# Attention kernel on one core: the dense product of a duo stands behind its last two maxima, and its copy behind the relu

## The reference, cut to what matters

```python
xn = layernorm(x)                                   # over the 256 columns
q = relu(xn @ Wq.T + bq)                            # keys k and values v likewise, once for all batches
score = einsum('bhsd,bhtd->bhst', qh, kh) / 4       # 16 heads of 16 columns
a = softmax(score) @ vh                             # then transposed to (head, d, s) and reshaped to 1024 x 256
w = (weights >= 0) * 2 - 1                          # a dense layer of signs
y = clip((xn @ w.T) * scale + bias, -100, 100)
out = x + (a + xn) + y
```

## Time and profile before

| | us |
|---|---|
| median of 3 runs | 2849.71 |
| lowest and highest | 2847.73, 2850.22 |
| the profiled execution's own time | 2850.59 |
| its span, first to last instruction | 2848.8 |
| PE busy | 2770.7 (97%) |
| ACT busy | 2450.2 (86%) |
| DVE busy | 2337.4 (82%) |
| POOL busy | 938.4 (33%) |

### The profile page before, as it was taken

The page is one execution under the profiler, slowest core; times in us unless marked ns, Lnnn a source line. Parts: engine busy times, 40 slices in busy tenths (PEclk is TensorE's granted clock), DMA queues, the critical chain, the costliest instruction groups (busy, mean ns, idle before and its releaser), DMA issues.

```text
span 2848.8 us, 61155 instructions
## 1 busy us (share of the span) xinstructions
PE 2770.7 (97%) x17860; PEld 1149.8 (40%) x17860; DVE 2337.4 (82%) x4578; ACT 2450.2 (86%) x2949; POOL 938.4 (33%) x845
## 2 busy tenths in 40 slices
PE   8899999999999999999999999999999999999996
PEld 4434444443444434444443444434444443444331
DVE  6788888888888888888888888888888888888940
ACT  4688888888888888888888888888888888888996
POOL 4304334242343314333242343314333242343001
PEclk8699999999999999999999999999999999999998
DMA  7111121121221121121121221121121121211111
GB/s 142 60 40 55 65 70 36 56 70 55 65 70 52 40 70 55 65 66 33 62 69 55 65 66 49 47 70 55 65 64 35 62 68 56 65 62 37 48 55 38
DMA packets 78637, 167.74 MB, mean 59 GB/s; under 512 B 28548, under 2 KB 32647, under 8 KB 76327
## 3 DMA queue, kind: packets, MB, share of 16 engines
q1 hardware_dynamic: 78374, 164.19, 19.2%
HBM read 36.71 MB, written 17.83 MB: 19 GB/s over the span
## 4 chain that ended last, share of the span: by engine, by line
PE 79%; issue 10%; DVE 7%; ACT 2%; POOL 1%; DVEq 0%; DMA 0%; POOLq 0%; ACTq 0%
PE value_ps L611 30%; PE ring L633 28%; PE score_ps L597 13%; DVE mx L959 5%; ACT probs L806 2%; PE score_ps L677 1%; PE score_ps L662 1%; PE score_ps L679 1%; PE score_ps L666 1%; PE score_ps L664 1%; PE ring L720 1%; POOL fin L1097 1%; PE score_ps L715 0%; DVE excess L934 0%; PE ring L700 0%
## 5 line engine op out<-in xcount | busy, mean ns | idle before, releaser
L806 ACT ACTIVATE probs<-score_ps 128x1024 f32<-128x1024 f32 x2048 | 1992.3, 1024 | 236.1 <-PE score_ps L597 229.9
L959 DVE TENSOR_REDUCE mx<-ring 128x1 f32<-128x512 f32 x2952 | 1900.1, 684 | 248.8 <-PE ring L633 224.5
L633 PE MATMUL ring<-kstack,qstack 48*128 48x512 f32 x3444 | 1168.4, 467 | 16.7 <-DVE mx L959 3.1
L611 PE MATMUL value_ps<-probs,vones 128*32 128x512 f32 x8192 | 1092.3, 605 | 1.1 <-ACT taken L813 0.4
L633 PEld LDWEIGHTS ring<-kstack,qstack 48*128 48x128 f32 x3444 | 490.1, 184 | 1071.0 <-DVE mx L959 1034.3
L597 PE MATMUL score_ps<-qstack,kstack 51*128 51x512 f32 x4096 | 814.1, 416 | 13.8 <-ACT probs L806 4.5
L934 DVE CUSTOM_DVE_ANT_0 excess<-ring,excess 128x512 f32<-128x512 f32 x512 | 353.1, 690 | 136.7 <-PE ring L633 119.1
L1097 POOL TENSOR_TENSOR dense<-dense,affine 128x512 f32<-128x512 f32 x128 | 164.4, 1284 | 866.7 <-ACT dense L856 865.2
L597 PEld LDWEIGHTS score_ps<-qstack,kstack 51*128 51x128 f32 x4096 | 393.6, 186 | 132.1 <-ACT probs L806 70.5
L822 ACT ACTIVATE excess<-ring 128x512 f32<-128x512 f32 x492 | 294.0, 597 | 1.4 <-PE ring L633 1.2
L611 PEld LDWEIGHTS value_ps<-probs,vones 128*32 128x32 f32 x8192 | 161.5, 108 | 320.7 <-issue 289.1
(11 more groups left out here) (93 smaller groups left out, 1417.2 us busy)
## 6 DMA issues: line engine op xcount, KB each, us to landing
qstack<-parts SPq DMA_DIRECT2D x768, 64.0 KB, 2.5
fin<-taken SPq DMA_DIRECT2D x256, 128.0 KB, 2.9
xin<-x SPq DMA_DIRECT2D x16, 1024.0 KB, 5.1
base_cur<-base_new SPq DMA_DIRECT2D x16, 1024.0 KB, 5.3
fin<-recip SPq DMA_DIRECT2D x32, 512.0 KB
out<-fin SPq DMA_DIRECT2D x32, 512.0 KB, 2.6
qstack<-proj SPq DMA_DIRECT2D x256, 12.0 KB
kstack<-base_cur SPq DMA_DIRECT2D x16, 128.0 KB, 6.0
```

The costliest lines, as they stand in the source:

```text
L611: mm = pe.matmul(value_ps[h4 * 32:(h4 + 1) * 32, :], vones[:, 2 * tp + c, hh * HALF + side * PAIRS + 2 * g + j, :, :], probs[:, q % 2 * GR ...
L633: pe.matmul(ps[:, :], qstack[nh][rows, pair, st * P:(st + 1) * P], keys, start=True, stop=True).then_inc(s_mm, 1)
L806: nc.scalar.activation(probs[:, q % 2 * GROUP + u % GROUP, :], score_ps[src][:, :], ACT.Exp, scale=EXP_SCALE).then_inc(s_probs, 1)
L959: nc.vector.tensor_reduce(most, src[:, :], AX.X, ALU.max).then_inc(s_mx, 1)
```

## The change

The tensor engine does the dense job after the two maxima "behind" instead of ahead of them, and the scalar engine makes the dense copy after the relu of the difference instead of ahead of it. Turn and project jobs, which are "between" jobs, stay where they are. Which bank and which score tile each product takes is not changed, since `plan` hands them out as before.

```diff
@@ half_step of the tensor engine
                     if last if d < 2 else att:
                         weigh(*(last if d < 2 else att), (d // 2 - 1) % QUADS, d % 2)
-                    if "behind" in at:
-                        do_job(b, hh, *job, at["behind"])
                     if now:
                         for n in behind:
                             maxima(b, hh, n, at)
                         if d == ROWS_DUO:
                             turn_maxima(b, hh, at["rows"])
+                    if "behind" in at:
+                        do_job(b, hh, *job, at["behind"])
@@ half_step of the scalar engine
                     if att:
                         exponentials(*att, 2 * d + 1, at["second"])
-                    if "behind" in at:
-                        take_job(b, hh, *job, at["behind"])
                     for n in itertools.chain(*maxima_of(d)):
                         if now and is_difference(n):
                             take_difference(b, hh, n, at)
+                    if "behind" in at:
+                        take_job(b, hh, *job, at["behind"])
```

## The result

The changed kernel takes 2852.64 us (median of 20 runs, 2851.16 to 2858.62), the kernel before 2848.93 us in the same comparison (20 runs, 2846.83 to 2852.98). The ratio is 1.0015, 95% interval 1.0009 to 1.0021: slower by 3.7 us, less than the 0.2% that was set as the bound of a difference, but clear of zero. A second comparison, on one chip, gave 1.0019 (1.0010 to 1.0028), 5.15 us between the medians.

A forecast was written before the change was run, and what follows sets the result against it. The tensor engine, busy for 97% of the span, was taken as the bound. 60 jobs at +0.06 us add 3.6 to the profiled 2850.59, giving 2854.2; the median lies 0.88 lower, so 2853.3 us, range 2845 to 2860.

The forecast's parts named there:

- Steps 1 to 3: Tensor engine: maxima 1 and 2 at E, first dense matmul 0.43 later, last at 1.37, a shift of 0.43.
- Steps 4 to 6: Dense copy 1.68 after E; second score pair, ready at 2.14, waits 0.19 for the copy and starts at 2.33.
- The cover of GpSimd: GpSimd's scaling of the copy ends some half a microsecond later, at no cost; without cover 7.5 us.
- Step 7: Vector engine no longer late for maximum 4; maxima 4 and 5 at 2.66, product with the values at 2.99.
- Step 8: Product with the values to the next block: 3.12 in the dense block, 3.13 in the projection block, the same.
- The sum: Values 2.99 after E against 2.93: +0.06 us for each of 60 dense jobs, 3.6 us in all.
- E: The moment the tensor engine leaves the even duo's product with the values; the prediction's times count from it.
- the marks of the two rivals: First dense matmul after E: 0.34 or less speaks for weights beside the maxima, 0.47 or more for the late bank.
- DVE's idle time split in two: Vector engine's 1.22 us of idle time before the reduction of maximum 1 was to be split in two.
- Weights beside the maxima: Dense weights load during the maxima, last dense matmul at 1.18: -0.13 us each, -7.8 us, 2841.9 us; chance 0.10.
- The late bank of maximum 2: Maximum 2 waits for its ring bank at E, the reduction of maximum 7: +0.13 each, +7.8 us, 2857.5; chance 0.24.
- The Trainium skill's rule of the draining switch: Changing tiling mode drains the tensor engine: by that rule alone 60 x 0.10 = 6 us slower, near 2856.

The follow-up runs named there:

- the short copy: Dense copy cut to 64 of 512 columns from batch 1 on: changed kernel 2835.17 us, ratio 0.9952 against before; kernel before 2848.64 us, 1.0001.
- the pair of short reductions: Maximum 1's reduction cut to 64 of 512 columns in dense blocks: kernel before 2841.84 us, ratio 0.9975; changed kernel 2852.62 us, 1.0016.
- on PE alone: Kernel before with only the dense product moved behind the maxima, its copy still ahead of the relu: 2868.21 us, ratio 1.0067.
- the version with the job between: Kernel before with dense jobs in duos 3, 5, 7 and 9, behind maximum 3, ahead of the second score pair: 2847.49 us, ratio 0.9996.

## Why the prediction was right

The forecast was 2853.3 us, +3.6; measured were 2852.64, +3.7, and +5.15 in the repeat. The gate, the shift and the wait that goes away were as forecast; that 3.6 and 3.7 agree to a tenth is luck, since the interval of the first comparison runs from 2.6 to 6.0 us and the 60 intervals with a job add up to 4.5 us in the repeat's trace. By its steps:

- Steps 1 to 3, the shift: 0.44 and 1.37 against 0.43 and 1.37. The hand-over from half-array to full-array products was read from a projection block, and held.
- Steps 4 to 6, the copy: 1.69 and 2.34 against 1.68 and 2.33. That it is the gate is shown by the short copy, 0.29 a job. The cover of GpSimd held: a batch in the loop loses 0.26 us, no more than its four jobs account for.
- Step 7, maxima and values: 2.68 and 3.01 against 2.66 and 2.99. That the vector engine had been the wait and is none now is shown by the pair of short reductions. What the prediction's account of before left out is the relu: it named maximum 4's bank alone as the 0.20, while the relu of maximum 2 ended at nearly the same time (722.46, the reduction of maximum 1 at 722.50). The change is cheap only because the relu moves ahead as well: without that, on PE alone, a job costs +0.32 and not +0.07. A small misreading is in it too: the four reductions overlap, so one takes 0.69 and not 0.645, and maximum 4 starts 0.05 and not 0.10 behind the end of its reduction; the sum doesn't change by it.
- Step 8, from the values to the next block: 3.13 as worked out.
- The sum: the four jobs of a batch in the loop cost 0.065 to 0.074 each, where 0.06 was said. In the last batch, outside the loop, they cost 0.18 each, not 0.06, and two duos with a dense job take 6.19 us there, which is past the prediction's own mark of 6.15; taking the last batch at the same price is the one term that was wrong. Here before, and then the repeat of the changed kernel, PE from the start of a block to the values:

```profile
2621.76 0.39 PE L677 MATMUL score_ps<-wf_sb,xnT_high 128*128 128x256 f32 x1
...
2624.63 1.07 PE L611 MATMUL value_ps<-probs,vones 128*32 128x512 f32 x8
```

```profile
2612.14 0.39 PE L677 MATMUL score_ps<-wf_sb,xnT_high 128*128 128x256 f32 x1
...
2614.11 0.50 PE L597 MATMUL score_ps<-qstack,kstack 51*128 51x512 f32 x2
2614.44 0.40 PE L633 MATMUL ring<-kstack,qstack 48*128 48x512 f32 x2
2614.77 1.06 PE L611 MATMUL value_ps<-probs,vones 128*32 128x512 f32 x8
```

Before, the values came 2.87 behind E and not 2.93. After, with E at 2611.72, they came at 3.05. So of the 0.12 that a job costs there beyond the forecast, half is that before was 0.06 quicker. The other half is the copy: it started at 2613.45, 0.37 behind the last dense matmul instead of 0.31. In the kernel before it started as late there (2622.69 to 2623.06), but was not the last wait. Why the hand-over is longer in the last batch, I did not find out. The repeat's trace has 3.8 us in the 56 intervals with a job in the loop and 0.7 in the last four, 4.5 against the 3.6 of the forecast: 0.5 of the difference is the last batch, 0.4 that a job in the loop costs nearly 0.07 and not 0.06.

The signs: blocks without a job stayed at 4.90 and the 60 waits for the copy stayed 60. The first dense matmul at 0.44 was right between the marks of the two rivals, 0.34 and 0.47. "DVE's idle time split in two" was wrong: the reduction of maximum 1 joins those ahead of it and the idle time lies in one piece behind.

The rivals. *Weights beside the maxima*: no trace shows it; the dense product waits for the end of the maxima less 0.07, here too. The Trainium skill's rule of weight loads pulled ahead ("TensorE: Matmul & The Clock Gate", "Step-by-step: what each phase is for") is not borne out across a change of shape: in the trace of after the weight load of the first dense matmul starts together with that matmul (725.11 and 725.12), while that of the second starts 0.11 ahead of its own. *The late bank of maximum 2*: it did not come late (both maxima at 724.68, directly behind the values). It is what happened elsewhere, though, with the reciprocal in duo 7 when the dense product no longer covered it. *The Trainium skill's rule of the draining switch* ("TensorEngine Tiling (Array Packing)", "Tiling Modes"): the trace agrees that a switch has a price, 0.33 for 0.23. The measured times alone don't rule out the 6 us that it was given (+3.7, +5.15, whose intervals reach 6.0 and 8.0). What speaks against it as the account of the sum is that the version with the job between has just as many switches as the changed kernel and its blocks are 0.2 us shorter, and that the short copy, with every switch in place, takes 0.29 us off a job.

## What to carry to other kernels

Work off the time of a moved job from its start to the last wait that now follows, in two columns, before and after, with every buffer's release in them; a stage where two releases end together gives back little if one of them goes. A job that covers another engine's hiccup is worth more than its place looks: before moving it, see what that engine does there. And put a job with a copy behind it where no product waits for the copied buffer: the same product cost 1.14 us behind the values, 1.21 behind the maxima (6.12 less 4.91) and 1.03 between (5.94 less 4.91), where no wait for the copy was left.

## What the runs showed of the hardware that I had not expected

- In the profiled execution of the changed kernel the granted clock fell to 0.50 for 10.2 us about 201 us into the span, behind an idle gap of PE of 1.33 us at the loop's start; the kernel before (1.34 us) and four of the other versions (1.31 to 1.33 us) had a like gap there and kept 1.00. What made it fall is open. It cost 4 us, about as much as the change.
- The next product of another shape started 0.07 before the modelled end of the last one in every pair that I read at the full clock: maxima to dense, dense to scores, scores and maxima to values. In these rows the hand-over can be worked out from a duration alone.
- The scalar engine's copy of 64 columns took 0.22 us and that of 512 columns 0.60, the vector engine's reduction 0.22 and 0.68 to 0.69.
